# A graph layer on one core: the 0/1 placing matrix made by ScalarE instead of VectorE, and a register loaded half a step earlier

## The reference

```
w = relu(edgefeats @ fnet_w1 + fnet_b1) @ fnet_w2 + fnet_b2   # 400000 edges, 13 -> 32 -> 256
W = w.reshape(-1, 16, 16)
inv_deg = 1 / max(segment_sum(1, edge_dst), 1)
for _ in range(2):
    xj = hx[edge_src]                          # 12500 nodes x 16
    m = einsum('ei,eio->eo', xj, W)
    agg = segment_sum(m, edge_dst) * inv_deg   # edge_dst is sorted
    hx = gru_cell(agg, hx)
out = layernorm(x + hx)
```

## Time and profile before

| | |
|---|---|
| three runs, median | 6458.52 us (6440.29 to 6484.48) |
| profiled execution, its own time | 6451.35 us |
| span of its trace | 6449.0 us |
| mean granted TensorE clock | 0.912 |
| PE busy | 5491.4 us, 85% |
| DVE busy | 4426.8 us, 69% |
| ACT busy | 3328.3 us, 52% |
| POOL busy | 3653.1 us, 57% |

### The profile page before, as it was taken

One profiled execution on the slowest core, in us unless ns is written; L12 is line 12 of the kernel. 1 busy time (PEld: TensorE's weight loads), 2 busy tenths in 40 slices (PEclk: granted clock), 3 DMA queues, 4 the chain that ended last, 5 costly groups with the idle time before them and its releaser, 6 DMA issues.

```text
span 6449.0 us, 124558 instructions
## 1 busy us (share of the span) xinstructions
PE 5491.4 (85%) x41939; PEld 4396.8 (68%) x41940; DVE 4426.8 (69%) x5962; ACT 3328.3 (52%) x5306; POOL 3653.1 (57%) x3867
## 2 busy tenths in 40 slices
PE   2888888888888888888877888888988888888887
PEld 1766666676676776666646777767777767777775
DVE  3866666666666666666656777777777777777776
ACT  1555555555555555555434555555555555555553
POOL 6355555555555555555546555555555555555553
PEclk7998999998999999999988999999999999999998
DMA  5111111111111111111111111111111111111110
GB/s 119 40 45 36 51 36 51 36 51 36 42 44 41 46 38 49 36 51 36 48 51 31 31 43 37 37 43 31 43 43 31 43 31 43 43 31 43 43 31 21
DMA packets 190346, 270.76 MB, mean 42 GB/s; under 512 B 90119, under 2 KB 158234, under 8 KB 176887
## 3 DMA queue, kind: packets, MB, share of 16 engines
q1 hardware_dynamic: 58779, 224.93, 10.4%
q0 software_dynamic: 123168, 31.78, 4.7%
q10 hardware_dynamic: 7838, 6.41, 0.4%
HBM read 202.89 MB, written 54.94 MB: 40 GB/s over the span
## 4 chain that ended last, share of the span: by engine, by line
PE 67%; issue 13%; another core or an unknown queue 10%; ACT 5%; DVE 3%; DVEq 1%; ACTq 0%; DMA 0%; SPq 0%
PE ps_all L838 40%; PE ps_all L850 8%; PE ps_all L840 6%; PE ps_all L825 4%; ACT src_hot L700 3%; PE ps_all L873 3%; PE ps_all L894 2%; PE ps_all L864 2%; ACT src_hot L704 1%; DVE shared L1303 1%; DVE fan L1263 1%; PE ps_all L880 1%; DVE xg L1311 0%; PE ps_all L899 0%
## 5 line engine op out<-in xcount | busy, mean ns | idle before, releaser
L838 PE MATMUL ps_all<-parts,src_hot 128*128 128x448 f32 x14478 | 3672.3, 390 | 245.6 <-issue 97.2
L838 PEld LDWEIGHTS ps_all<-parts,src_hot 128*128 128x128 f32 x14478 | 2848.5, 199 | 639.3 <-issue 289.3
L628 POOL DMA_INDIRECT xg<-in_x,idx x1973 | 1868.6, 947 | 1435.5 <-issue 510.8
L628 POOL DMA_INDIRECT xg<-h_rows,idx x1876 | 1770.1, 944 | 1258.6 <-issue 474.8
L1303 DVE TENSOR_TENSOR shared<-ps_all,at_hot 128x448 f32<-128x448 f32 x2413 | 1406.7, 618 | 1499.8 <-PE ps_all L840 824.2
L700 ACT ACTIVATE src_hot<-keys,neg_key 128x384 fp32r<-128x384 int16 (+1 forms) x3088 | 1687.8, 619 | 1218.7 <-remote 578.5
L1311 DVE TENSOR_REDUCE xg<-shared 128x48 f32<-128x1344 f32 (+1 forms) x772 | 1244.3, 1612 | 82.0 <-DVE shared L1303 2.3
L704 ACT ACTIVATE src_hot<-src_hot 128x1536 fp32r<-128x1536 f32 (+1 forms) x772 | 1190.0, 1541 | 71.4
L1263 DVE TENSOR_TENSOR fan<-xg,ps_all 128x1280 f32<-128x1280 f32 x784 | 1159.5, 1479 | 40.7 <-issue 19.4
L850 PE MATMUL ps_all<-fan,h_sb 128*32 128x160 f32 x12544 | 742.5, 310 | 230.3 <-issue 209.8
L840 PE MATMUL ps_all<-parts,src_hot 128*128 128x448 f32 x2413 | 909.0, 377 | 13.1 <-issue 12.8
(11 more groups left out here) (134 smaller groups left out, 1368.3 us busy)
## 6 DMA issues: line engine op xcount, KB each, us to landing
keys<-key_d SPq DMA_DIRECT2D x98, 832.0 KB
h_d<-h_sb SPq DMA_DIRECT2D x49, 1056.0 KB
h_sb<-h_d SPq DMA_DIRECT2D x49, 1056.0 KB
xg<-in_x,idx POOLq DMA_INDIRECT x1973
xg<-h_rows,idx POOLq DMA_INDIRECT x1876
ef<-in_ef_t SPq DMA_DIRECT2D x49, 420.0 KB
acc_all<-agg_t SPq DMA_DIRECT2D x1, 3161.0 KB
idx<-in_src_tiles SPq DMA_DIRECT2D x98, 32.0 KB
```

The costliest lines, as they stand in the source:

```text
L628: pool.indirect_dma_start(out=xg[:, buf, at, 0:C], out_offset=None, in_=rows_of, in_offset=bass.IndirectOffsetOnAxis(ap=idx[:, buf, at:at ...
L838: pe.matmul(ps_g[j], src_hot[k % 2][:, kb, j * P:(j + 1) * P], parts[:, m * WHOLE + kb, :], start=(kb == 0 and m == 0), stop=False)
```

## The change

`places` goes from VectorE to ScalarE. It is split in `places_far`, four Abs activations a call (at k = 1 and k = 2, after the half's copies, before `keep_turned`), each of 144 columns with one column of `slot_of` as its bias, and `places`, one Relu over all 1152 columns (at k = 3). For the last super of a round, all of it comes at k = 6 of that super; before, VectorE did it there too. `slot_of` is kept with its sign changed, so that it can be added as a bias.

The load of `more` goes to the start of half 7 on TensorE, ahead of `products`, and into half 6 on VectorE, between `add_windows` and `pick_rows`. Only the first super of round 0 keeps it at the end. The branch stays where it was.

```diff
+            def places_far(rnd, s, sup, part):
+                if part == 0:
+                    act.wait_ge(s_slots, 1)
+                    wait_pos(act, s_sc, scattered(rnd, s, 0) - 1)
+                for b in range(part * BPS, (part + 1) * BPS):
+                    act.activation(place[:, b, :], iota[:], ACT.Abs,
+                                   bias=slot_of[:, bass.ds(s * 2 * BPS + b, 1)]).then_inc(s_place_far, 1)
+
+            def places(sup):
+                act.wait_ge(s_place_far, 2 * BPS * (sup + 1))
+                act.activation(place[:], place[:], ACT.Relu, bias=1.0, scale=-1.0).then_inc(s_place, 1)
...
+                        if k in (1, 2) and not is_first(i, par):
+                            places_far(rnd, 2 * i + par - 1, sup - 1, k - 1)
                         if k == 2 and not is_first(i, par):
                             keep_turned(sup - 1, 1 - buf)
+                        if k == 3 and not is_first(i, par):
+                            places(sup - 1)
+                        if k == 6 and is_last(i):
+                            places_far(rnd, NSUP - 1, sup, 0)
+                            places_far(rnd, NSUP - 1, sup, 1)
+                            places(sup)
...
                     for k in range(HPS):
+                        if k == 7 and not (is_first(i, par) and rnd == 0):
+                            more = pe.value_load(meta[0:1, bass.ds(s + 2 * NBLK, 1)],
+                                                 min_val=0, max_val=N // XWIN + 1)
...
-                link(dve.tensor_scalar(slot_of[:], slot_of[:], lane[:, 0:1], None, ALU.add))
+                dve.tensor_scalar(slot_of[:], slot_of[:], lane[:, 0:1], -1.0, ALU.add, ALU.mult).then_inc(s_slots, 1)
...
-            def places(rnd, s):
-                wait_pos(dve, s_sc, scattered(rnd, s, 0) - 1)
-                dve.tensor_tensor(place[:], iota_ps.unsqueeze(1).to_broadcast([P, 2 * BPS, SPAN]),
-                                  slot_of[:, bass.ds(s * 2 * BPS, 2 * BPS)].unsqueeze(2).to_broadcast(
-                                      [P, 2 * BPS, SPAN]),
-                                  ALU.is_equal).then_inc(s_place, 1)
...
-                        if k == 6 and is_last(i):
-                            places(rnd, NSUP - 1)
+                        if k == 6 and not (is_first(i, par) and rnd == 0):
+                            more = dve.value_load(meta[0:1, bass.ds(s + 2 * NBLK, 1)],
+                                                  min_val=0, max_val=N // XWIN + 1)
...
-                        if not is_first(i, par):
-                            if k == 2:
-                                places(rnd, s - 1)
```

More of the change, by code:

```diff
@@ L344, in gnn_program @@
         s_agg_t = sem("s_agg_t")
+        s_slots = sem("s_slots")
+        s_place_far = sem("s_place_far")
         s_place = sem("s_place")
@@ L963, in emit @@
                         pe.wait_ge(s_more, 1)
-                    more = pe.value_load(meta[0:1, bass.ds(s + 2 * NBLK, 1)],
-                                         min_val=0, max_val=N // XWIN + 1)
+                        more = pe.value_load(meta[0:1, bass.ds(s + 2 * NBLK, 1)],
+                                             min_val=0, max_val=N // XWIN + 1)
                     with pe.If(more > 0):
@@ L1388, in emit @@
                         dve.wait_ge(s_acc, 32)
-                    more = dve.value_load(meta[0:1, bass.ds(s + 2 * NBLK, 1)],
-                                          min_val=0, max_val=N // XWIN + 1)
+                        more = dve.value_load(meta[0:1, bass.ds(s + 2 * NBLK, 1)],
+                                              min_val=0, max_val=N // XWIN + 1)
                     with dve.If(more > 0):
```

## The result

The change made the kernel slower: 6568.71 us at the median of 4 runs (6532.52 to 6581.26) against 6449.41 us of the kernel before beside it (4 runs, 6424.69 to 6484.48). The ratio is 1.017, with a 95% interval of 1.0107 to 1.0236. The profiled execution took 6581.26 us with a span of 6579.5, 130 us more than that of before. It is the slowest of the four, so what is read from the two traces is some 11 us more than the 119 us between the medians.

What follows compares the result with a forecast made beforehand. The prediction took TensorE to bound the kernel. From the profiled 6451.35 us it took 8 for the matrix leaving VectorE and added 7 for late `place`, giving 6450; the forecast was 6452 us, range 6390 to 6520.

Steps and rivals of the forecast that it cites:

- What bounds the kernel: TensorE, busy 85% of the span; largest idle groups "issue" at L864 (272.8 us) and L850 (209.8 us).
- its own sign of being wrong: Wrong if "issue" at L864 and L850 moves over 10%, src_hot's 74.4 us grows, or Abs starts are 0.5 us or more apart.
- The matrix leaves VectorE: Round 1, half 3's gather: 0.17 us wait behind the matrix goes in 47 supers, 8 us gained; bounds 0 and 41 us.
- The matrix on ScalarE: 355 us more ScalarE time; late `place` delays the scatter in 14 of 47 round-0 supers, costing 7 us.
- The slower rival: `place` becomes the scatter's last wait if Abs starts are over about 0.45 us apart: 101 us, 6552 us, chance 0.12.
- TensorE's load: Load ahead of half 7 is covered by queued matmuls, at least 2.7 us ahead of the next products: worth 0.
- VectorE's load: Load in half 6 between window adds and picks costs 0, at most 0.4 x 96 = 38 us.
- The cover named: VectorE's 8.62 us of idle in the half after half 6, taken to hide its load: cost 0.
- The faster rival: At a super's head, sequencers arrive 0.7 us earlier and L864's "issue" shrinks: 67 us gained, 6384 us, chance 0.15.

Runs made afterwards that it cites:

- f2: The kernel before, unchanged, run for its trace on a chip where it takes some 4985 us: 4987.0 us, one run.
- e1: Kernel before with only the placing matrix moved to ScalarE, both loads of `more` as before: 4984.56 us, ratio 1.000.
- e3: Kernel before with only TensorE's load of `more` moved ahead of half 7: 4983.22 us, ratio 1.000.
- i2: Kernel before with only TensorE's load of `more` ahead of half 7, run again: 4983.47 us, ratio 1.000.
- j2: Kernel before with only TensorE's load of `more` ahead of half 7, run once more: 4992.97 us, ratio 1.000.
- e2: Kernel before with both loads of `more` moved ahead as in the change, matrix still on VectorE: 5006.84 us, ratio 1.004.
- e4: Kernel before with only VectorE's load of `more` moved into half 6: 5006.24 us, ratio 1.004.
- i3: The change with TensorE's load of `more` back at the end of the super: 5007.32 us, ratio 1.005 to the kernel before.
- k1: The change with TensorE's load of `more` back at the end of the super, run again: 5008.47 us, ratio 1.004 to the kernel before.
- h1: The change with VectorE's load of `more` in half 4 instead of half 6: 6621.03 us, ratio 1.019 to the kernel before.
- h2: Kernel before with the matrix on ScalarE, each Abs cut into four of 36 columns, loads as before: 6571.4 us, ratio 1.010.
- h3: Kernel before with VectorE's load of `more` in half 6, done twice: 6579.36 us, ratio 1.011.
- i1: Kernel before with only the placing matrix moved to ScalarE, both loads as before, run again: 4984.57 us, ratio 1.000.
- group 3: The runs of h1, h2 and h3 on one chip, 3 rounds, with the kernel before beside them at 6510.07 us.
- f1: The change unaltered, on a chip where the kernel before takes 4985.22 us: 5003.74 us, ratio 1.004.

## Why the prediction was wrong

It said no change, 6452 us and at most 6520; it was 6569. By its own steps:

- **What bounds the kernel**: TensorE, and "issue" its largest wait; that was so, but the sum then took "issue" for a fixed cost. The two groups that it named did stay within 10% (272.8 to 256.5, 209.8 to 219.8), so its own sign of being wrong didn't show. The group at the aggregate, 28.5 us before and 100.4 after, it never listed. This is the step that failed: the sum has no term for what the edits do to these stretches and to the clock in and behind them, and it needed one of about 120 us (119 between the medians, 130 between the traces).
- **The matrix leaves VectorE**, 8 us: right on the chip it was read from. Halves 2 and 3 of round 1 took 5.68 + 6.70 = 12.38 us before and 5.59 + 6.59 = 12.18 after, 0.20 x 47 = 9 us, and the gather of half 3 starts 0.68 us after the products instead of 0.86 (medians). On a fed chip it is 0.68 already in the kernel before (f2), and nothing is gained: e1 is 1.000. VectorE's busy time fell by 114 us and not by 132, mostly since its instructions overlap: in the earlier trace rows the matrix lasts until 4545.67 and the fan starts at 4545.59.
- **The matrix on ScalarE**: an Abs has 409 ns (0.42 estimated), and the trace of ACT in round 0 has four of them in 1.32 us, as laid out:

```profile
2102.05 0.39 ACT L665 ACTIVATE h_sb<-ps_all 128x264 f32<-128x264 f32 x1
2102.33 1.32 ACT L714 ACTIVATE place<-iota,slot_of 128x144 f32<-128x144 f32 x4
2103.71 2.14 ACT L702 ACTIVATE src_hot<-keys,neg_key 128x384 fp32r<-128x384 int16 x4
```

  The Relu has 1165 ns (1.19 estimated). ScalarE's busy time grew by 327 us (355). The late `place` cost 16.2 us where 7 was taken, 12.3 of it in 19 supers of round 0 (14 had been laid out), or up to 41 with what the trace may hide. Right in mechanism, at least 9 us short. Some 3 of them are the step from ScalarE to TensorE: the scatter starts 0.25 us after the Relu's end in each of these waits, where 0.1 was taken. The slower rival, `place` as what the scatter waits for, didn't happen: its price of 101 us needed 0.45 us from start to start, and it was (1.32 - 0.41)/3 = 0.30. That the time landed beside that rival's 6552 is chance.
- **TensorE's load**, 0: right on fed chips (e3, i2, j2). On short chips not settled, see below.
- **VectorE's load**, 0, with 0.4 x 96 = 38 us as its bound: mis-sized. The cover named, 8.62 us of idle in the next half, lay behind the load, not between it and the pick that the gather waits for. It costs 18 to 22 us on a fed chip (e2, e4, i3, k1), all from halves 6 and 7 of round 1, where the margin is 0.2 us. On a short chip it stays nearly unseen in the wait (68.0 before, 75.6 after): the picks of these two halves end 3.7 and 2.3 us ahead of the gather in the trace of before (medians), where f2 has 0.2.
- **The faster rival** was about the right place, the head of a super, with the wrong sign. It expected TensorE's sequencer to gain by coming there earlier. The Trainium skill, "Runtime: NRT & Kernel Launch", Instruction fetch mechanics, was used there to say that the branch stays and nothing is gained; the trace agrees that nothing was gained, and no run shows whether that mechanism is at work.

**What is shown and what is open.** Shown: the loss on a short chip lies in stretches in which TensorE crawls while no engine keeps it waiting, and in the clock in and behind them; in the result's pair of traces half 0 of round 0's supers alone has 47 x 2.44 = 115 us of it, and half 0 of round 1's 47 x 1.73 = 81, while other halves give back and lose; the late `place` doesn't make it (16 us, at most 41); it doesn't need VectorE's load in half 6 (h1 has the loss with that load in half 4); where TensorE is fed the same change costs 0.4%, and all of that is VectorE's load. Open: which edit lengthens the stretches on a short chip. For TensorE's load speaks that in round 0 the long head comes with it and not without it, in five traces. Against it: in round 1 h1 has the load and no long head; in no trace is it the only edit; and h2 and h3, without it, lose 1.0% and 1.1% (in round 0 h2 is longer in halves 1 and 4, h3 in 1, 5 and 6). It may be that any shift of the work moves and lengthens such stretches, as those two did away from the head; that is theory S, and it is untested too. The kernels that would part them, i1 to i3, were never on a short chip: they ran in groups 1 and 4 to 6, all fed.

## What to carry to other kernels

When the largest wait of the bounding engine has no releaser, it isn't a constant: here small edits moved the time by 119 us (medians) in a kernel with 699 us of such waits, where the direct waits that they touched were worth 8 and 16 us. The range has to hold that, and the small groups of such waits are to be listed with the large. Here a load of a register was priced by the margin of the very next instruction on its engine that the bounding engine waits for, not by idle time later in its row: moving it two halves made 0.4% into nothing. And when a kernel's time differs this much between two groups of runs, a verdict on a few edits belongs to the condition in which it was measured.

## What the runs showed of the hardware

The kernel before took 4985 to 4995 us in groups 1, 2 and 4 to 7, on four chips, and 6449 to 6510 beside the result and in group 3, with equal work on VectorE, ScalarE and GpSimd. In the traces the difference is TensorE's "issue" time (19 us against 723) and its clock: mean granted 0.990 against 0.912, that is, all but 97 us at 2.4 GHz on the fed chip, and 1,133 us at 1.2 GHz on the short one. In the slow stretches there TensorE goes on in steps of 0.68 to 0.75 us, 437 of them counted in the kernel before and none in f2. What makes a chip short is not known from these runs: the load of a register took the same (305 ns in f1, 311 in the earlier trace rows), a packet of the larger instruction queue did too (1.00 and 1.01 us), and so did VectorE's picks (618 ns) and GpSimd's gathers (947 ns) in the traces of before and f2. The short traces also lack a quarter of the updates by the engines' instructions, which the fed ones have; whether that belongs to the same cause isn't known.
